# Attention and a low-rank feed-forward block on one core: denominators' copy one unit up, the first maximum in the projection, output operands fetched in the last pair, the last division moved, loops written out

## The reference

```python
x = x + attn(layernorm(x)) @ W_out          # 16 heads of 64, causal softmax over 2048 tokens
x = x + layernorm(x) @ (W + up_aux @ lora_up @ lora_down @ down_aux).T + b

def attn(x):
    q, k, v = split(x @ W_qkv, 3)            # W_qkv is 256 x 3072
    score = q @ k.T / 8, masked above the diagonal
    return softmax(score) @ v
```

## Time and profile before

| | |
|---|---|
| runs | 2073.56, 2072.45, 2081.17 us (median 2073.56) |
| the profiled execution's own time | 2072.66 us |
| its span from first to last instruction | 2070.9 us |
| TensorE busy | 1845.7 us (89%), granted clock 0.964 of full on the mean |
| VectorE, ScalarE, GpSimd busy | 1213.9, 802.0, 1059.2 us |
| 16 DMA engines | 171.48 MB, mean 83 GB/s |

### The profile page before, as it was taken

How to read it: one execution, slowest core, us unless ns; L and a number is a source line. 1 busy time by engine, 2 the same in 40 slices (tenths; PEclk the granted TensorE clock), 3 DMA queues, 4 the chain that set the end, 5 groups by cost and what they waited for, 6 DMA issues and landing times. The chain is left out here.

```text
span 2070.9 us, 39060 instructions
## 1 busy us (share of the span) xinstructions
PE 1845.7 (89%) x13464; PEld 1120.0 (54%) x13464; DVE 1213.9 (59%) x2071; ACT 802.0 (39%) x981; POOL 1059.2 (51%) x575
## 2 busy tenths in 40 slices
PE   6999976898989898899989989988898989995898
PEld 5888853544545444454444444544454545452797
DVE  4434337757575666575756666675757576721565
ACT  3222221344444343434444443534344434353331
POOL 0000000667665757575756666576666576755111
PEclk9999985999999999999999999999999999998899
DMA  5555452212121212112121212121212121011651
GB/s 192 210 198 208 187 183 75 64 38 73 42 63 44 62 47 62 53 52 68 43 63 42 67 38 73 52 73 35 70 42 62 44 63 51 17 37 36 249 183 51
DMA packets 150792, 171.48 MB, mean 83 GB/s; under 512 B 44618, under 2 KB 91744, under 8 KB 150624
## 3 DMA queue, kind: packets, MB, share of 16 engines
q1 hardware_dynamic: 150624, 169.15, 25.4%
HBM read 97.02 MB, written 71.57 MB: 81 GB/s over the span
## 5 line engine op out<-in xcount | busy, mean ns | idle before, releaser
L840 DVE TENSOR_REDUCE b_part_max<-b_ring 128x1 f32<-128x512 f32 (+2 forms) x1226 | 687.1, 603 | 431.9 <-PE b_ring L660 324.3
L782 ACT ACTIVATE b_probs<-b_scores 128x1024 f32<-128x1024 f32 (+3 forms) x640 | 568.7, 898 | 903.4 <-PE b_scores L632 518.1
L944 POOL TENSOR_TENSOR b_sum_pool<-b_sum_pool,b_probs 128x1024 f32<-128x1024 f32 x288 | 684.4, 2376 | 116.8 <-ACT b_probs L782 102.0
L701 PE MATMUL b_o_acc<-b_probs,b_v_in 128*64 128x512 f32 (+3 forms) x2560 | 550.0, 551 | 0.0
L660 PE MATMUL b_ring<-b_k_hi,b_q_hi 64*128 64x512 f32 (+2 forms) x1226 | 276.4, 446 | 123.5 <-ACT b_den_row L798 81.2
L660 PEld LDWEIGHTS b_ring<-b_k_hi,b_q_hi 64*128 64x128 f32 x1226 | 118.8, 189 | 345.7 <-DVE b_part_max L840 176.1
L632 PE MATMUL b_scores<-b_q_hi,b_k_hi 64*128 64x512 f32 (+2 forms) x1280 | 273.5, 422 | 18.8 <-ACT b_probs L782 13.6
L701 PEld LDWEIGHTS b_o_acc<-b_probs,b_v_in 128*64 128x64 f32 x2560 | 158.0, 138 | 232.8 <-issue 169.0
L944 POOL TENSOR_TENSOR b_sum_pool<-b_probs 128x1024 f32<-128x1024 f32 x48 | 115.6, 2408 | 293.5 <-ACT b_probs L782 293.5
L632 PE MATMUL b_scores<-b_q_hi,b_k_lo 64*128 64x512 f32 (+2 forms) x1280 | 238.4, 367 | 0.0
L632 PE MATMUL b_scores<-b_shift,p_first_row 64*128 64x512 f32 (+2 forms) x1280 | 237.7, 366 | 0.0
(11 more groups left out here) (115 smaller groups left out, 2012.7 us busy)
## 6 DMA issues: line engine op xcount, KB each, us to landing
b_raw<-k_t SPq DMA_DIRECT2D x32, 512.0 KB, 4.6
b_raw<-q_t SPq DMA_DIRECT2D x32, 512.0 KB, 5.4
b_v_in<-v SPq DMA_DIRECT2D x16, 1024.0 KB, 5.3
b_recip<-r_t SPq DMA_DIRECT2D x128, 128.0 KB, 2.9
o_t<-b_o_norm SPq DMA_DIRECT2D x64, 256.0 KB, 2.0
c_o_in<-o_t SPq DMA_DIRECT2D x7, 2048.0 KB, 9.2
q_t<-a_stage_a SPq DMA_DIRECT2D x32, 256.0 KB, 2.0
q_t<-a_stage_d SPq DMA_DIRECT2D x32, 256.0 KB, 2.0
```

What stands on the lines that cost most here:

```text
L701: last = nc.tensor.matmul(o_acc[head(h), off:], v_in[u][:, j, head(h)], probs[s % PR][:, h, off:], start=(j == 0), stop=(j == NB * t + NB ...
L782: nc.scalar.activation(probs[s % PR][:, :, off:], scores[s % 2][:, :, off:], ACT.Exp, scale=scale).then_inc(exp_done, 1)
L840: nc.vector.tensor_reduce(part_max[:, h, ib, c:c + 1], rowwise[h][:, 0:width], AX.X, ALU.max).then_inc(chunk_reduced, 1)
L944: nc.gpsimd.tensor_tensor(sum_pool[:], first, probs[s % PR][:], ALU.add).then_inc(pool_added, 1)
```

## The change

In six parts:

- The constants are filled on POOL inside the projection's block; the block of their own is gone.
- Item 0's loads of q, k and v, the split, the 40 chunks, their maxima and the placing of the maxima in `shift` run inside the projection. The groups get 4 PSUM banks in place of 6, and the chunks two. From token tile 2 on a chunk stands behind every second group; one reduction takes both heads. SP loads item 1's first operands at the start of the attention (before, item 0's split freed the buffers for them earlier).
- ACT copies the denominators at unit start + 3.
- In item 15 SP fetches tiles 0 and 1 of o_t, ACT casts W_out and the four parts of tile 0, DVE takes the low halves.
- The division of the very last query tile leaves the attention: its denominators are multiplied after tile 0's output projection, SP runs its five transfers there before it loads tiles 2 and 3, and POOL divides ahead of its bias additions.
- The loops of PE, ACT, DVE and SP, and POOL's in the attention, are written out.

```diff
-    BANKS = 6
+    BANKS = 4
+    LOADED_AT, CAST_AT, CHUNKS_FROM = 14, 6, 11
+    for p in range(LOADS):
+        T, g = max((PIECE_TILES * (p + 1), CHUNKS_FROM), after)
+        for k in range(CH):
+            if chunks[k][0] * P // PIECE == p:
+                chunk_at[T, g] = k
+                T, g = (T, g + 2) if g + 2 < GROUPS else (T + 1, 1)
+        after = (T, g)
...
+                def chunk_products(k):
...
+                    pe.wait_ge(lead["split_hi"], 2 * (ib * P // PIECE + 1))
+                    if k:
+                        pe.wait_ge(lead["chunk_reduced"], 2 * k)
+                    for h in range(2):
+                        last = nc.tensor.matmul(rowwise[:, h, 0:wide], q_hi[head(h), ib * P:(ib + 1) * P],
+                                                k_hi[head(h), c * TILE:c * TILE + wide], start=True, stop=not diagonal)
...
+                        if (T, g) in chunk_at:
+                            chunk_products(chunk_at[T, g])
...
                         for late in late_tile(n, s - 1, previous):
                             copy_o(*late)
-                        for late in late_tile(n, s - 4, previous):
+                        for late in late_tile(n, s - 3, previous):
                             copy_denominators(*late)
...
-                item(0, 0, True, False)
-                with pe.Fori(0, PAIRS - 1) as pair:
-                    item(pair, 1, True)
-                    item(pair + 1, 0, True)
-                item(PAIRS - 1, 1, False)
-                denominators(LAST_ITEM, TI - 1, LAST_ITEM, [ring_last[ring_banks["denom", TI - 1][0]]])
+                for n in range(2 * PAIRS):
+                    item(n // 2, n % 2, n < LAST_ITEM, n > 0)
...
+        WO_SLOTS = (4, 5)
+        PART_SLOTS = [U - 16 + 3 * p for p in range(PARTS)]
...
+                            if s in WO_SLOTS:
+                                weights_high(WO_SLOTS.index(s))
+                            if s in PART_SLOTS:
+                                first_high(PART_SLOTS.index(s))
...
-                sp.wait_ge(o_lo_ready, PARTS)
+                finish_last_o()
+
+                wait_apart(sp, o_lo_ready, PARTS, first_loaded[0], 16)
                 load_o(2, 0, slice(0, KC), o_loaded[0])
                 step(0, 0, True, True, False)
...
                 norm(0, 0, 1)
-                with dve.Fori(0, halfway - 1) as i:
+                dve.wait_ge(tail["den_moved"], o_tiles * 32 + 1)
+                nc.vector.reciprocal(tail["recip_spread"][:], tail["den_spread"][:]).then_inc(tail["inverted"], 1)
+                for i in range(halfway - 1):
```

More of the change, by code:

```diff
@@ L30 @@
 EPS = 1e-5
+LOADS = 2
+PARTS = 4
 LOWEST = -3.0e38
@@ L82, in project_qkv @@
     assert GROUPS % BANKS == 0 and HALF % STAGES == 0 and tiles % 2 == 0 and BANKS % 2 == 0
+    D = P // 2
+    KB = L // P
+    PIECE = L // LOADS
+    PIECE_TILES = PIECE // TILE
+    head = lambda h: slice(h * D, (h + 1) * D)
+    chunks = [(ib, c) for ib in range(KB) for c in range(ib // NB + 1)]
+    CH = len(chunks)
+    K_GROUP = QK // 2
+    LOADED_AT, CAST_AT, CHUNKS_FROM = 14, 6, 11
+    chunk_at, diff_at, after = {}, {}, (0, 0)
+    for p in range(LOADS):
[5 more added lines that the diff above has]
+        after = (T, g)
+    TURN_AT = after
+    PLACE_AT = (after[0] + 1, 2)
+    assert TURN_AT < (tiles - 1, 0) and PIECE_TILES * LOADS < tiles
     ctx = ExitStack()
@@ L150, in tile @@
                             sp.dma_start(x_in[u][:], rows).then_inc(x_loaded[u], 16)
[L152 to L158, removed]
+                for T in range(tiles):
+                    tile(T, T % 2, T + 2 < tiles)
                 for e in range(2):
@@ L202, in tile @@
                         group(T, u, g, first)
+                        if (T, g) in chunk_at:
+                            chunk_products(chunk_at[T, g])
+                        if (T, g) == TURN_AT:
+                            turn_first_max()
                         if ahead and g == 12:
                             transposes(T + 1, 1 - u)
+                pe.wait_ge(constants, CONSTANTS)
                 transposes(0, 0)
[L207 to L211, removed]
+                for T in range(tiles):
+                    tile(T, T % 2, T + 1 < tiles, T == 0)
             def empty(eng, e, T, g):
@@ L1155, in _ @@
                 last.then_inc(l_made, 1)
-                with pe.Fori(0, halfway - 1) as i:
-                    step(i * 2 + 1, 1)
-                    step(i * 2 + 2, 0)
-                step(tiles - 1, 1)
+                pe.wait_ge(tail["den_copied"], o_tiles + 1)
+                for T in range(1, tiles):
+                    step(T, T % 2)
                 transposes(tiles - 1, 1)
```

478 lines of the change are left out of this document (292 added, 186 removed).

## The result

The changed kernel takes 1957.6 us (median of 4 runs, 1955.1 to 1958.35) against 2073.01 us for the kernel before in the same session: a ratio of 0.9436, 95% interval 0.9407 to 0.9465, so 115 us less. The forecast was 1927 us, 145 less, with a range of 1893 to 1980. The direction and most terms held; 30 us of the gain did not come.

A forecast was written before the change was run, and what follows sets the result against it. PE was taken as the bound in the projection, with a gap, attention waits and an end chain behind it; terms from -74 (copy) and -59.1 (gap) to +27.6 (projection) sum to -145.3, so 2072.66 becomes 1927 us, range 1893 to 1980.

The forecast's parts named there:

- Constants, projection, gap: Constants filled under the first load, -4.6 us; first maximum inside the projection, +27.6; gap before the first score, -59.1.
- PE held for each reduction, +52: Rival, projection: each of 40 chunks holds PE for a whole 1.3 us reduction, 52 us more, 1979 us; chance 0.1.
- Start of the attention: First scores: a shorter half-clock stretch, -1.2 us; ACT's cast of item 1's late-loaded k and q, +3.
- The copy, -74: Attention: denominators' copy one unit up cuts 81.2 us of PE waits to 7, 0.15 left in each of 44.
- the wait changes its name: Rival, attention: DVE's late reductions keep 53 us of the waits, and 24 of half-clock stretches stay; 2004 us, chance 0.1.
- The half-clock stretches, -24: Attention: 14 stretches of 3.41 us at half clock, 1.7 lost in each, go with PE's pauses for the denominators.
- The rival that rested on it: Rival, attention: the half-clock stretches have another cause than the 2 us pauses and stay, 24 us back; 1951 us, chance 0.1.
- Loops, -9: Attention: writing out the loops saves 1.5 us of PE idling at each of six branches; nothing in the projection.
- the rival of 2101 us: Rival: straight code starves PE of instructions, 116 transfers at 1.5 us cost 174, so slower at 2101 us; chance 0.03.
- Last item, +3: Item 15: DVE's six subtractions, 7.2 us, compete with POOL's additions; bounds 0 and 7 us, +3 taken.
- Last stage, -7: Output projection: starts 24.5 us sooner, but PE waits 15 us for tile 2's load behind the last division; -7 us.
- does not wait for tile 2: Rival, last stage: tile 2's load lands in time, so 15 us of stall and the half clock go; 1910 us, chance 0.07.

## Why the prediction was right in most and wrong in one term

*Constants, projection, gap.* -4.1, +27.6 and -59.0 against -4.6, +27.6 and -59.1. The largest terms were sound because each was the length of a visible stretch or a count times a duration of a row. Inside the projection's 27.6 the shares were not tested by a run; only their sum is confirmed, and that it fits to a tenth is partly luck, since it held 2 us for waits that PE's busy time does not show. Its rival (PE held for each reduction, +52) did not come: PE is busy for 296.69 of 296.70 us.

*Start of the attention.* The forecast had a short half-clock stretch that costs 1.7 us; it was 13.65 us long, reaching into item 0's first units, with PE busy for 9.36 of it. ACT's wait for item 1's operands was 2.84 us (forecast 3). All in all -0.5 against about -3.

*The copy, -74.* This is the step that failed, and in one sentence of it: "I leave 0.15 us of new wait in each of 44". The copy is worth 72 us in the looped kernel and 49 in the straight one. The missing 23 us are 1.6 in each of items 1 to 14. Of these 1.2 are lost at the first tile change, where DVE's sum of 256 columns takes 2.56 us in place of 0.42; the other 0.4 stay open. I had asked whether POOL keeps up with PE and whether DVE was free at the bank that I looked at. I had not asked what a copy taken out of ACT's list does to the moment at which POOL starts. That the lock costs PE this is shown by the run that only changes POOL's wait: the 1.2 us are gone from that chunk. That run also takes away two losses per item that the kernel before had, so its 31.5 us is not a measure of this one alone.

*The rival "the wait changes its name"* put 53 us back and kept the half-clock stretches. Of its two halves one came in part, 23 us, of which 17 by the lock and not by the pace of the reductions, and the other did not come. It deserved more than 0.1.

*The half-clock stretches, -24.* All 14 went, as forecast; item 15 has a new one behind its pause of 3.0 us. The reason given was not the whole of it: written-out loops alone take 12 of them away with 73.8 us of the waits still there, and the copy alone leaves 4. Items 1 to 14 of the kernel before hold 42 pauses at the copy, 14 of 2.04 us from start to start and 28 of 2.24. Only 14 of the 42 have a stretch behind them, 9 of the shorter and 5 of the longer. Written out, 14 take 1.83 us, with 2 stretches, and 28 take 2.02, with none; with the copy up in the looped kernel, the 4 stand behind 2.16 to 2.30 us at the loop's head. So the stretches went with the pauses, but what makes one pause bring a stretch and the next not stays open, and that all 14 would go was a better guess than its reason. The Trainium skill, "TensorE: Matmul & The Clock Gate", on oscillation, puts the fall of the clock down to longer idle gaps than these and would have kept the stretches. The traces do not agree: the kernel before has its 14 behind such pauses, and the changed kernel, whose pauses in items 1 to 14 are 1.43 us at most, has none there. The rival that rested on it falls.

*Loops, -9.* -6.6, from the run with the loops alone, after the stretches are taken out. No pause came with straight code, so the rival of 2101 us falls.

*Last item, +3.* +8.6. I had priced the subtractions against POOL's additions, and left out what the new loads do in SP's queue: they wait for a store to land and hold the denominators' transfer, DVE waits for that in order, and PE for DVE's sums. Turning that order round took 4 us from the item in its profile. The rest lies at the item's end: POOL's last addition ends at 1786.70 and DVE's last sum at 1790.42, 8.6 us behind PE's last product with v, where the kernel before had 5.0. Which share of these 3.6 belongs to the subtractions of o no run took apart.

*Last stage, -7.* -8.2, and its mechanism was right in each link: the pause ahead of tile 2 was 14.2 us where the forecast had 15. The test with the load ahead gave the 15 us that the rival "does not wait for tile 2" spoke of.

The attention, 1474.4 us, stayed just under the 1475 that I had named as the mark of being wrong, and the output projection began at 1790.9 in place of about 1760: some 22.6 us from items 1 to 14, 2.5 from the attention's start and 5.6 from the last item.

## What to carry to other kernels

When an edit takes work out of one engine's list, ask what starts earlier on the engines that it feeds, and whether an order that used to fall right by a tenth of a microsecond now falls wrong; where two engines compete, fix the order with a semaphore on data that is there anyway, which costs nothing if the one that waits has slack. Before placing a load that waits for something into a queue, list what stands behind it and who waits for that, since in-order engines pass the delay on three times. And the gains of two edits that each remove the same side effect, here the half-clock stretches, do not add.

## What the runs showed of the hardware that I had not expected

- DVE's addition of two SBUF operands of 128x256, 0.42 us long, takes up to 2.57 us when POOL's addition starts 0.1 us ahead of it, and 0.41 when it starts 0.08 us behind. In the changed kernel that is 1817 ns against 417 on the mean of 64, some 90 us of DVE's time.
- Stretches of 3.41 us at half clock (1.2 GHz) far from a stage's edge stand behind pauses of some 2 us on PE, but not behind each: 14 behind 42 pauses of 2.04 or 2.24 us in the kernel before, 2 behind 42 of 1.83 or 2.02 with the loops written out. In the changed kernel, with no pause over 1.43 us in items 1 to 14, there is none in them.
- After 3.5 us without a product at the start of the attention, 13.65 us were at half clock in the changed kernel. In the other kernels with the same start of the attention it was 6.8 to 13.65 us in all, in one piece or two.
